# Eight experts as one sequence of 128 tiles: downs four tiles behind ups, a ring of eight, one split in four on GpSimd, side steps one chunk ahead

## What is computed

```python
router_weights = softmax(xf @ rw + rb)
topw, topi = top_k(router_weights, 2)
topw = softmax(topw)
combine = zeros((T, E)).at[arange(T)[:, None], topi].add(topw)
h = gelu(einsum('td,edf->etf', xf, w1) + b1[:, None, :])      # E=8, D=128, F=512
eo = einsum('etf,efd->etd', h, w2) + b2[:, None, :]
out = einsum('etd,te->td', eo, combine)
x = layernorm(x + out, ln3_g, ln3_b)
```

## Time and profile before

| | us |
|---|---|
| median of 3 runs | 1045.59 (1045.52 to 1046.74) |
| the profiled execution | 1047.26 |
| its span, first to last instruction | 1045.5 |
| busy in the span: PE | 869.4 (83%) |
| PEld | 530.6 (51%) |
| DVE | 762.1 (73%) |
| ACT | 612.3 (59%) |
| POOL | 519.7 (50%) |
| the expert layer, first up to end of the span | 822.5 to 1045.5 |

### The profile page before, as it was taken

The page is one execution under the profiler, slowest core; times in us unless marked ns, Lnnn a source line. Parts: engine busy times, 40 slices in busy tenths (PEclk is TensorE's granted clock), DMA queues, the critical chain, the costliest instruction groups (busy, mean ns, idle before and its releaser), DMA issues.

```text
span 1045.5 us, 23536 instructions
## 1 busy us (share of the span) xinstructions
PE 869.4 (83%) x8314; PEld 530.6 (51%) x8314; DVE 762.1 (73%) x1680; ACT 612.3 (59%) x1487; POOL 519.7 (50%) x1045
## 2 busy tenths in 40 slices
PE   3798988974555878998998899998988788888895
PEld 1344444443333545555755456565555466565664
DVE  4888888978775655665566766677476788989886
ACT  0877777858885213554355456664555566666674
POOL 2677777875553424763444556655344322323313
PEclk9999556555555989999999899999999999999998
DMA  9400000000000000000000010000000000000000
GB/s 263 154 1 2 0 0 1 2 1 0 1 2 1 1 0 1 2 2 2 1 2 2 24 25 22 24 23 14 2 1 2 1 1 2 2 12 0 10 2 21
DMA packets 23573, 16.39 MB, mean 16 GB/s; under 512 B 8744, under 2 KB 20400, under 8 KB 23344
## 3 DMA queue, kind: packets, MB, share of 16 engines
q1 hardware_dynamic: 23472, 15.06, 5.0%
HBM read 10.85 MB, written 1.05 MB: 11 GB/s over the span
## 4 chain that ended last, share of the span: by engine, by line
PE 50%; DVE 26%; ACT 10%; issue 8%; POOL 4%; DMA 1%; DVEq 1%; SPq 0%; ACTq 0%; POOLq 0%
ACT sb_E L1243 6%; PE ps_context L784 5%; DVE sb_neg_raw L1542 4%; PE ps_context L787 3%; PE ps_scores L860 3%; DVE sb_E L1970 3%; PE ps_scores L884 3%; DVE sb_inv_den L1785 2%; POOL sb_E L2267 2%; PE ps_scores L676 2%; PE ps_scores L737 2%; PE ps_scores L777 2%; PE ps_turned L1088 2%; DVE sb_neg_half L1753 2%; PE ps_turned L698 2%
## 5 line engine op out<-in xcount | busy, mean ns | idle before, releaser
L1243 ACT ACTIVATE sb_E<-ps_scores,sb_neg_max,sb_score_scale 128x256 f32<-128x256 f32 (+1 forms) x384 | 190.9, 515 | 60.0 <-DVE sb_neg_max L1545 59.6
L2267 POOL TENSOR_SCALAR sb_E<-sb_E,sb_inv_sum 128x256 f16<-128x256 f32 x256 | 123.5, 482 | 43.4 <-DVE sb_inv_sum L1582 25.3
L1496 ACT ACTIVATE sb_E<-ps_scores,sb_ff_bias 128x512 f32<-128x512 f32 x128 | 87.6, 688 | 66.6 <-PE ps_scores L1129 64.2
L1146 PE MATMUL ps_turned<-sb_moe_down,sb_E 128*128 128x128 f16 x512 | 92.6, 220 | 23.9 <-DVE sb_E L1970 23.8
L1970 DVE TENSOR_TENSOR sb_E<-sb_E 128x512 f16<-128x512 f32 x128 | 93.1, 745 | 23.4 <-ACT sb_E L1499 21.2
L1753 DVE TENSOR_REDUCE sb_neg_half<-ps_scores 128x16 f32<-128x1024 f32 x48 | 58.7, 1222 | 68.3 <-PE ps_scores L860 68.3
L1542 DVE TENSOR_REDUCE sb_neg_raw<-ps_scores 128x4 f32<-128x1024 f32 (+1 forms) x80 | 97.3, 1217 | 13.4 <-PE ps_scores L676 11.7
L1565 DVE TENSOR_REDUCE sb_neg_quad<-ps_scores 128x2 f32<-128x512 f32 (+1 forms) x96 | 64.5, 686 | 42.0 <-PE ps_scores L739 30.0
L1148 PE MATMUL ps_turned<-sb_moe_down,sb_E 128*128 128x128 f16 x512 | 92.1, 219 | 0.0
L1147 PE MATMUL ps_turned<-sb_moe_down,sb_E 128*128 128x128 f16 x512 | 92.1, 219 | 0.0
L2202 POOL TENSOR_SCALAR sb_veps<-sb_mv 128x2 f32<-128x2 f32 x72 | 17.4, 241 | 149.0 <-DVE sb_mv L1525 144.7
(11 more groups left out here) (285 smaller groups left out, 2260.5 us busy)
## 6 DMA issues: line engine op xcount, KB each, us to landing
sb_moe_up<-in_moe_up SPq DMA_DIRECT2D x1, 2048.0 KB
sb_KS<-sb_qk_parts SPq DMA_DIRECT2D x96, 16.0 KB, 1.8
sb_QS<-sb_qk_parts SPq DMA_DIRECT2D x96, 16.0 KB, 1.8
sb_rows<-in_rows SPq DMA_DIRECT2D x1, 1216.0 KB, 7.8
out_x<-sb_raw_context SPq DMA_DIRECT2D x8, 128.0 KB, 1.8
sb_X<-in_x SPq DMA_DIRECT2D x1, 768.0 KB, 9.9
sb_square<-in_square SPq DMA_DIRECT2D x1, 768.0 KB, 11.0
sb_ctxT<-in_ctxT SPq DMA_DIRECT2D x1, 512.0 KB, 11.2
```

The source lines that it names most:

```text
L1146: pe.matmul(dst, u_hi, hi, start=(first and i == 0), stop=False, skip_group_check=True)
L1243: last = act.activation(E[:, ring, head], SC[t % 2][:, head], ACT.Exp, bias=neg_max[:, ring, h:h + 1], scale=scale, accum_out=row_sum[:, r ...
L1496: last = act.activation(U_full[:, k % 4, :], banks[k % 4], ACT.Gelu, bias=bias, scale=1 / WEIGHT_SCALE)
L2267: last = pool.tensor_scalar(E16[:, ring, SEQ * h:SEQ * h + SEQ], E[:, ring, SEQ * h:SEQ * h + SEQ], inv_sum[:, ring, h:h + 1], HALF, ALU.m ...
```

## The change

The experts run as one sequence of 128 tiles without chunk ends; all loops of the layer are written out. `down(n - 4)` follows `up(n)`. `U_full` and `U_parts` become rings of eight (`RING`), the extra room coming from other layers' tiles (E, KBD); `h_parts` and `combine_down` get two buffers, and `final_z` moves. For tiles with k % 4 == 3 GpSimd makes the low part (`lower`) instead of VectorE, with a semaphore of its own. Routing of chunk c + 1 runs wholly within chunk c (tiles 19 to 31; chunk 0's own in tiles 1 to 7), and the other side steps move to earlier tiles, each some tiles behind what it reads. The takes stand one tile later on VectorE (k % 4 == 0), the last two of a chunk in the next chunk.

```diff
-HI_BY_VECTOR = 1
+HI_BY_VECTOR, LO_BY_POOL = 1, 3
+BEHIND, RING = 4, 8
+FIRST_ROUTING, NEXT_ROUTING = (1, 2, 3, 5, 7), ((27, 28, 29, 30, 31), (25, 26, 27, 29, 31))
...
-        h_parts = KBD[:, 0, 0:2 * CHUNK].rearrange("p (s k) -> p s k", s=2)
-        U_parts = E16[:, :, :].rearrange("p r (s k) -> p r s k", s=2)
+        h_parts = KBD[:, 0, 0:4 * CHUNK].rearrange("p (b s k) -> p b s k", b=2, s=2)
+        U_parts = (*(E16[:, i, :] for i in range(4)), *(KBD[:, 1, UNIT * i:UNIT * i + UNIT] for i in range(4)))
...
                 def down(c, k):
...
-                    wait(pe, S["split"], B["split"] + n + 1)
+                    if k % 4 == LO_BY_POOL:
+                        pe.wait_ge(S["split_p"], B["split_p"] + n // 4 + 1)
+                    else:
+                        pe.wait_ge(S["split"], B["split"] + n - n // 4 + 1)
...
+                def tile(n):
+
+                    c, k = divmod(n, L.tiles)
+                    if n >= 2:
+                        up(c, k)
+                    if k == (12 if c == 0 else 4):
+                        turn_combine(c)
+                    if k == (17 if c == 0 else 10):
+                        expert_bias(c)
+                    if k == 11 and c < NCHUNK - 1:
+                        chunk_turn(L, B, c + 1)
+                    if k == (23 if c == 0 else 18) and c < NCHUNK - 1:
+                        router(c + 1)
...
-                chunk(0, True)
-                with pe.Fori(1, NCHUNK - 1) as c:
-                    chunk(c, True)
-                chunk(NCHUNK - 1, False)
+                for n in range(NCHUNK * L.tiles + BEHIND):
+                    if n < NCHUNK * L.tiles:
+                        tile(n)
+                    if n >= BEHIND:
+                        down(*divmod(n - BEHIND, L.tiles))
```

On ScalarE, in place of the wait for four tiles back:

```diff
+                    if n >= RING:
+                        act.wait_ge(S["down"], B["down"] + n - RING + 1)
```

On VectorE, in place of `chunk(c, following)`:

```diff
+                def tile(c, k):
+
+                    following, ended = c < NCHUNK - 1, c > 0
+                    if k % 4 != LO_BY_POOL:
                         split(c, k)
+                    if k in (0, 4) and ended:
+                        take(c - 1, EXPERTS - 2 + k // 4)
+                    if k % 4 == 0 and k > 4:
+                        take(c, k // 4 - 2)
+                    if c == 0 and k in FIRST_ROUTING:
+                        routing(c, FIRST_ROUTING.index(k) + 1)
+                    if k in (1, 2) and following:
+                        norm_stats(B, 2 * c + 2 + k - 1, k - 1)
+                    if k == (12 if c == 0 else 5):
+                        dve.wait_ge(S["logits"], 3 * c + 2)
+                        dve.tensor_copy(combineT[:, :], CO[0:EXPERTS, :]).then_inc(S["routed"], 1)
+                    if k in (6, 7) and following:
+                        wait(dve, S["x_based"], B["x_based"] + 2 * c + 1 + k - 6)
+                        norm_apply(B, 2 * c + 2 + k - 6, k - 6)
+                    if k in (9, 10) and ended:
+                        final_stats(c - 1, k - 9)
+                    if k == (18 if c == 0 else 11):
+                        add_bias(c)
+                    if k == 13 and following:
+                        tokens(c + 1)
+                    if k == 14 and following:
+                        token_parts(c + 1)
+                    if k == 15 and following:
+                        token_rest(c + 1)
+                    if k in (18, 21) and ended:
+                        final_norms(c - 1, (k - 18) // 3)
+                    if k == (23 if c == 0 else 19) and following:
+                        routing(c + 1, 0)
+                    if k in NEXT_ROUTING[c > 0] and following:
+                        routing(c + 1, NEXT_ROUTING[c > 0].index(k) + 1)
```

On GpSimd:

```diff
+                def lower(n):
+
+                    u, hi, lo = U_full[:, n % RING, :], U_parts[n % RING][:, 0:CHUNK], U_parts[n % RING][:, CHUNK:]
+                    pool.wait_ge(S["act"], B["act"] + n + 1)
+                    pool.tensor_tensor(lo, u, hi, ALU.subtract).then_inc(S["split_p"], 1)
+
+                route_exp(0, route[:, 1, :], route[:, 2, :], EXP1)
                 for c in range(NCHUNK):
...
+                    for k in range(LO_BY_POOL, L.tiles, 4):
+                        if k == 7 and c == 0:
+                            route_exp(c, route_s[:, 4, :], route_s[:, 5, :], EXP2)
+                        if k == L.tiles - 1 and c < NCHUNK - 1:
+                            route_exp(c + 1, route_s[:, 4, :], route_s[:, 5, :], EXP2)
+                        lower(L.tiles * c + k)
+                        if k == 3 and c < NCHUNK - 1:
+                            for b in range(2):
+                                inverse_std(B, 2 * c + 2 + b, b)
+                        if k in (7, 15) and c < NCHUNK - 1:
+                            base(L, B, 2 * c + 2 + k // 8, k // 8)
+                        if k == 11 and c > 0:
+                            final_inverses(c - 1)
+                        if k == (23 if c == 0 else 19) and c < NCHUNK - 1:
+                            route_exp(c + 1, route[:, 1, :], route[:, 2, :], EXP1)
+                        if k in (23, 27) and c > 0:
+                            finish(c - 1, (k - 23) // 4)
+                final_inverses(NCHUNK - 1)
+                for u in range(2):
+                    finish(NCHUNK - 1, u)
```

159 lines of the change are left out of this document (53 added, 106 removed).

## The result

The changed kernel takes 1036.27 us (median of 20 runs, 1031.77 to 1045.69) against 1045.66 of the kernel before (20 runs beside them): ratio 0.9912, 95% interval 0.9893 to 0.993. It is faster by 9.4 us where 20.6 were forecast, and 1036.27 lies just beyond the far end of the range. The direction was right and the size was not: the prediction was wrong.

The account below looks back on a forecast made before the run. TensorE's 34 us of waits, mainly for VectorE's splits, were to shrink until VectorE binds the middle chunks. Savings of 2.5 + 6.6 + 6.6 + 4.4 = 20.1 us from 1047.26, median 1.67 lower, gave 1025 us; range 1015 to 1036.

Parts of the forecast that it names:

- a quarter of the low halves to GpSimd: Expert layer: moving 8 splits a chunk saves VectorE 4.8 us, and conflict with GpSimd costs it 4.8 us again.
- The share: Part of the 8.0 us a chunk upper bound for which GpSimd's splits hold VectorE: 0.6 taken, 4.8 us.
- rival C: Total conflict: every GpSimd split costs VectorE 1.0 us, every side add 0.72; middle chunk 53.9 us, 1041 us; chance 0.15.
- VectorE 47.8 us, so a chunk of 47.7: Chunks 1 and 2: VectorE's summed time exceeds TensorE's 45.1 us and sets the chunk's length, saving 6.6 us each.
- the side adds keep their 2.4: Middle chunks: GpSimd's side adds go on stretching VectorE's splits by 2.4 us a chunk.
- busy time under 44 or over 51 us: Sign that the forecast is wrong: VectorE's busy time in a middle chunk outside these limits.
- Free while VectorE is under 1.5 us late, else up to 1.4 us of stall a chunk: GpSimd's queue: the split of tile 23, behind the 5.44 us power, starts 1 to 2 us after its input, 3.3 allowed.
- The 1032 us: Kernel time if GpSimd's splits hold VectorE fully (share 1, 8.0 us a chunk), with a middle chunk of 51.0 us.
- VectorE is far below TensorE: Chunk 3: with no next chunk to route TensorE binds, 45.2 us against 49.63, 4.4 us saved.
- the walk: Start of chunk 0, new order stepped through with the old durations: TensorE waits about 4.7 us in place of 5.7.
- B (TensorE binds): VectorE keeps step and conflicts fall into free slots: chunks of 45.1 us, 27.8 us saved, 1018 us; chance 0.22.
- D's mechanism: GpSimd's and VectorE's in-order queues wait for each other; at 1.5 us in all eight groups a chunk, 1057 us; chance 0.08.

Follow-up runs that it names:

- experiment 1: The changed kernel with all low halves on VectorE, none on GpSimd: 1025.43 us, ratio 0.9794 to the kernel before.
- experiment 2: The changed kernel with GpSimd's low-half subtraction cut to 8 of 512 columns, its waits and order kept: 1019.50 us.
- experiment 11: High halves of k % 4 == 1 by ScalarE: changed kernel without splits on GpSimd 1018.31 us (0.9738), with them 1026.89 us (0.9813).
- experiment 6, second kernel: The changed kernel with low halves of tiles 7 and 15 back on VectorE, 23 and 31 still on GpSimd: 1030.78 us, ratio 0.9851.
- experiments 3 and 4: The changed kernel with GpSimd's powers replaced by multiplications: 1023.60 us; the same with all low halves on VectorE too: 1020.94 us.

## Why the prediction was wrong

**Right: what can go, and by what.** Of the 34 us of waits, 20.1 were to go with the whole change; sequence, distance and side steps save 21.8 by themselves (experiment 1), with eight splits a chunk more on VectorE. TensorE's floor of 45.1 us is 45.03 in two kernels. ScalarE stayed cover at 35.9 us and even at 40.5. The waits ahead of first downs fell from 23.8 us to 13.0 (5.9 + 4.0 + 3.1 in the view of waits), where near 10 was forecast.

**The step that failed: "a quarter of the low halves to GpSimd", priced at nothing.** The prediction set 4.8 us of conflict a chunk against 4.8 saved. The runs put 12.0 us on it (ratios: 0.9912 against 0.9794, 12.3 us; 8.8 at equal clock). It failed in three ways, the second the heaviest.
- *The share.* 0.6 was taken; 0.78 at least was measured (experiment 2). The rows chosen, VectorE's splits beside GpSimd's adds, were long operations. The new pairing also catches links of 0.19 us, and holds each for nearly a microsecond. Sizes aren't what is held; instructions are. Against rival C I had set routing, takes and reductions aside as operations that "read one SBUF tensor or are short". For takes and reductions that held; the routing's two-input links took the largest part, 2.9 to 3.5 us a chunk.
- *The place.* The forecast turned busy time into chunk time: VectorE 47.8 us, so a chunk of 47.7. VectorE's busy time came out at 47.0, the chunk at 49.85. A held link in a chain that another engine waits for is not load but delay. Experiment 11 shows it with the prediction's own share: VectorE is held for 4.8 us a chunk, is busy for 41.5 us under a floor of 45.1, and the splits still cost 9.6 us (8.0 at equal clock). That VectorE's 47.0 us came so near the 47.3 is luck. The 2.4 us of stretch by the side adds, "the side adds keep their 2.4", went with the new order (experiment 1: 44.23 us with all splits on VectorE, where 44.9 was its own work without stretch), and the hold was larger by about as much. So the sign set for being wrong, busy time under 44 or over 51 us, stayed silent.
- *The queue.* "Free while VectorE is under 1.5 us late, else up to 1.4 us of stall a chunk" was named and left out of the sum. It is 1.66 us in both middle chunks: 3.3 us, to which the power's 5.95 us instead of 5.44 adds its part. It too is lateness added up: with two splits fewer it is gone, the split of tile 23 still behind the power (experiment 6, second kernel).

**Against rows of before.** The split of GpSimd let VectorE go after 1.0 us in the earlier trace rows, and after 1.0 us here too. The Trainium skill (SBUF — State Buffer, "Who interferes with whom") has a VectorE operation with two SBUF inputs, or one in a two-port mode, exclude a GpSimd operation that reads SBUF for the whole instruction. The trace agrees for GpSimd's subtracts and adds, links on 128x4 included, and again not for the power: four VectorE splits beside the one at 905.90 took 0.68 to 0.69 us each. The 1032 us that the prediction worked out by that rule was nearer to the 1036.27 than my 1025, and still short, because busy time was again taken for chunk time.

**Chunk by chunk** (waits saved against forecast): chunk 0 -0.4 against 2.5; chunks 1 and 2 4.4 and 4.9 against 6.6; chunk 3 0.8 against 4.4. The forecast for chunk 3, "VectorE is far below TensorE", held for its load (38.41 us) and missed that it begins with the last seam of the routing: 2.4 us at tile 4, 0.5 at tile 3, and 1.5 by the low clock after it. In chunk 0 the first wait (3.3 us at tile 6, split 2 behind the routing behind the first power) was in the walk as 4.7 us for all of the start; the second, 4.1 us at the turn, was not, nor was the 1.6 us of clock. The tail is 9.7 us, 9.90 before, in the same order as said.

**The rivals.** B (TensorE binds) came true only without the splits and with VectorE relieved (experiment 11). C (total conflict) had the hold of the splits nearly right, 0.78 of it or more, and the side adds wrong: 53.9 us for VectorE in all against 47.0. D's mechanism, two in-order queues waiting for each other, is what the seam shows, at two or three places a chunk instead of eight groups. So the true case was C's hold with D's places, which no rival had; each alone was priced, not the two together, and by experiments 3 and 4 the mix adds some 3 us at equal clock (8.1 with the falls).

**What stays open.** How the 12 us divide between hold and queue: taking away the hold gives 15.8 us (14.2 at equal clock), the powers 11.4 (8.2), two splits of eight 4.5 to 8.3 (4.5 to 6.7), and none of these add up. How often the clock falls in executions that were not profiled, and so what part of the ratios it is. Also why the unchanged part before the layer differs by up to 8 us from trace to trace.

## What to carry to other kernels

Moving an instruction from a late engine to an idle one isn't paid in the idle engine's time: ask what it locks while it runs, what stands ahead of it in that in-order queue, and which chain of short operations will meet it. An operation of 0.19 us held for nearly 1 us in a chain that crosses engines can cost more than its share of busy time, so add such holds to the path, not to the load. A busy time that comes out as forecast doesn't show that its terms were right. And when a wait can be answered by taking work off an engine, look for the engine whose work doesn't hold it up: ScalarE took eight casts a chunk for 4 to 6 us of gain (layers 191.3 and 186.9, ratios 0.9794 and 0.9738), GpSimd eight splits for 12 of loss. Last, look at the clock of each window before two layers are compared: one fall is 1.6 us.
